# A hand-laid order of steps laid out anew, and the last half-tile stored from ScalarE's queue

## The reference

```
x = x + tanh(g_xattn) * autocorrelation(layernorm(x), ctx, ctx)
x = x + tanh(g_ffn)   * ffn(layernorm(x))

autocorrelation, per batch, 8 heads of 64 features, over the 64 tokens:
    corr = ifft(fft(q) * conj(fft(k))).real        # q = layernorm(x), k = v = ctx
    w, idx = top_k(corr, 8); w = softmax(w)        # per feature
    out[pos] = sum_i w[i] * v[min(idx[i] + pos, 63)]
ffn:
    out = (silu(x @ W_gate.T) * (x @ W_up.T)) @ W_down.T      # 512 -> 1792 -> 512, f16 weights
```

## Time and profile before

| | |
|---|---|
| Time, median of 3 runs | 213.95 us (213.7 to 213.95) |
| Profiled execution: first to last instruction | 212.1 us |
| Granted TensorE clock, mean | 1.000 |
| PE busy | 203.6 us (96%) |
| DVE, ACT, POOL busy | 135.7, 131.4, 122.4 us |

### The profile page before, as it was taken

How to read it: one execution, slowest core, us unless ns; L and a number is a source line. 1 busy time by engine, 2 the same in 40 slices (tenths; PEclk the granted TensorE clock), 3 DMA queues, 4 the chain that set the end, 5 groups by cost and what they waited for, 6 DMA issues and landing times.

```text
span 212.1 us, 6601 instructions
## 1 busy us (share of the span) xinstructions
PE 203.6 (96%) x2700; PEld 147.8 (70%) x2700; DVE 135.7 (64%) x408; ACT 131.4 (62%) x207; POOL 122.4 (58%) x151
## 2 busy tenths in 40 slices
...
DMA packets 20734, 17.89 MB, mean 84 GB/s; under 512 B 16096, under 2 KB 16992, under 8 KB 20320
## 3 DMA queue, kind: packets, MB, share of 16 engines
...
HBM read 10.65 MB, written 2.10 MB: 60 GB/s over the span
## 4 chain that ended last, share of the span: by engine, by line
PE 89%; DVE 5%; ACT 1%; DMA 1%; issue 1%; POOL 1%; DVEq 0%; POOLq 0%
PE psum L937 48%; PE psum L1121 23%; PE psum L920 6%; PE psum L1071 3%; PE psum L928 2%; PE psum L1056 2%; DMA x_sb<-x 1%; PE psum L1048 1%; PE psum L1014 1%; DVE top L792 1%; DVE probs L814 1%; DVE raw_stats L759 1%; PE psum L1016 1%; PE psum L1015 1%; DVE prod L782 1%
## 5 line engine op out<-in xcount | busy, mean ns | idle before, releaser
L937 PE MATMUL psum<-xt_hi,wu 128*128 128x128 f16 (+1 forms) x504 | 54.0, 213 | 0.0
L937 PE MATMUL psum<-xt_lo,wu 128*128 128x128 f16 (+1 forms) x504 | 54.0, 213 | 0.0
L937 PE MATMUL psum<-xt_hi,wg 128*128 128x128 f16 (+1 forms) x504 | 54.0, 213 | 0.0
L937 PE MATMUL psum<-xt_lo,wg 128*128 128x128 f16 (+1 forms) x504 | 53.9, 213 | 0.0
L632 POOL TENSOR_TENSOR hid_lo<-hid,hid_hi 128x512 f16<-128x512 f32 (+2 forms) x32 | 33.6, 1055 | 28.8 <-ACT hid_hi L750 28.7
L937 PEld LDWEIGHTS psum<-xt_hi,wg 128*128 128x128 f16 x504 | 44.8, 98 | 5.6 <-issue 5.0
L937 PEld LDWEIGHTS psum<-xt_hi,wu 128*128 128x128 f16 x504 | 45.0, 98 | 3.2 <-issue 2.4
L937 PEld LDWEIGHTS psum<-xt_lo,wu 128*128 128x128 f16 x504 | 45.1, 98 | 0.7
L937 PEld LDWEIGHTS psum<-xt_lo,wg 128*128 128x128 f16 x504 | 45.0, 98 | 0.6
L1121 PE MATMUL psum<-wd,hid_hi 128*128 128x512 f16 (+1 forms) x126 | 43.3, 356 | 0.0
L1121 PE MATMUL psum<-wd,hid_lo 128*128 128x512 f16 (+1 forms) x126 | 43.3, 355 | 0.0
...
## 6 DMA issues: line engine op xcount, KB each, us to landing
...
```

Source lines behind the costliest of these rows:

```text
L937: last = nc.tensor.matmul(psum[:, bank, a * n:(a + 1) * n], w[:, k, m * P:(m + 1) * P], xt[:, e, k, tok], start=(k == 0 and part == 0), st ...
```

## The change

The text `ORDER` is replaced. The set of steps is the same, with one more, `store_half:7`. PE's sequence is the same up to `kspec:2`; the other engines' sequences differ from the start. The beginning, one later place of the new text and both ends:

```diff
-warm:0 stats1:0 rstd1:0 kspec:0 q_norm:0 kcopy:0 qspec:0 kcopy:0.1 vspec:0 prod:0 stats1:1 lags:0 vcopy:0
-vcopy:0.1 prod:0.1 rstd1:1 kspec:1 max:0 lags:0.1 warm:0.1 sub:0 kcopy:1 sub8:0 match:0 exp8:0 exp:0 total:0
-vcopy:1 mask:0 max:0.1 kcopy:1.1 scale:0 sub8:0.1 wt:0 stats1:2 exp8:0.1 w_hi:0 match:0.1 gates:0 wspec:0
-q_norm:1 total:0.1 scales:0 sub:0.1 qspec:1 mix_prod:0 exp:0.1 mix_prod:0.2 mix:0 prod:1 mix:0.1 mask:0.1
-prod:1.1 residual:0 lags:1 k_hi:3 scale:0.1 rstd2:0 max:1 wt:0.1 rstd1:2 w_hi:0.1 sub:1 xn:0 wspec:0.1 match:1
+warm:0 stats1:0 rstd1:0 kspec:0 q_norm:0 kcopy:0 qspec:0 kcopy:0.1 vspec:0 prod:0 stats1:1 lags:0 vcopy:0 prod:0.1
+vcopy:0.1 rstd1:1 kspec:1 max:0 sub:0 q_norm:1 lags:0.1 sub8:0 match:0 exp8:0 exp:0 total:0 warm:0.1 vcopy:1 mask:0
+max:0.1 kcopy:1 scale:0 sub8:0.1 sub:0.1 exp8:0.1 wt:0 total:0.1 exp:0.1 match:0.1 w_hi:0 kcopy:1.1 wspec:0 stats1:2
+mask:0.1 gates:0 rstd1:2 qspec:1 mix_prod:0 mix_prod:0.2 mix:0 q_norm:2 scales:0 prod:1 mix:0.1 prod:1.1 scale:0.1
+lags:1 residual:0 wt:0.1 rstd2:0 max:1 w_hi:0.1 k_hi:3 sub:1 wspec:0.1 xn:0 match:1 xt:0 sub8:1 mix_prod:0.1 kspec:2
...
+residual:5 scale:6 gate:4.2 kcopy:7 w_rows_hi:6 rstd2:5 vcopy:7 up:4.1 h_hi:4 w_rows_lo:6 xn:5 up:4.2 hid:4.1
+tanh:4.2 q_lo:7 w_t:6.1 kcopy:7.1 silu:4.2 h_lo:4 w_t:6 gate:4.3 h_hi:4.1 hid:4.2 h_lo:4.1 up:4.3 store:3 tanh:4.3
...
-hid:7.2 up:7.3 h_hi:7.2 tanh:7.3 h_lo:7.2 down:7 silu:7.3 hid:7.3 h_hi:7.3 h_lo:7.3 down:7.1 down:7.2 down:7.3
-out:7 store:7
+silu:7.3 down:7 h_hi:7.2 h_lo:7.1 h_lo:7.2 hid:7.3 down:7.1 h_hi:7.3 h_lo:7.3 down:7.2 down:7.3 out:7 store:7
+store_half:7
```

The store of the right half leaves SP for ScalarE's queue, with a semaphore of its own:

```diff
                 if step == "store":
-                    for h, cols in enumerate(halves(p)):
-                        sp.wait_ge(out_ready, p + h + 1)
-                        sp.dma_start(outv[:, p:p + 1, cols], x_sb[:, p:p + 1, cols]).then_inc(stored, 16)
-            sp.wait_ge(stored, 16 * (PAIRS + 1))
+                    cols = halves(p)[0]
+                    sp.wait_ge(out_ready, p + 1)
+                    sp.dma_start(outv[:, p:p + 1, cols], x_sb[:, p:p + 1, cols]).then_inc(stored, 16)
+            sp.wait_ge(stored, 16 * PAIRS)
+            sp.wait_ge(half_stored, 16)
...
+                if step == "store_half":
+                    act.wait_ge(out_ready, PAIRS + 1)
+                    nc.scalar.dma_start(outv[:, p:p + 1, halves(p)[1]], x_sb[:, p:p + 1, halves(p)[1]])\
+                      .then_inc(half_stored, 16)
```

```diff
-    w_whole = sb("w_whole", [P, 2, D])
+    w_whole = v_turned[:, 0, :, :]
...
-    xt_hi = sb("xt_hi", [P, 2, KT, P], f16)
+    xt_hi = sb("xt_hi", [P, 4, KT, P], f16)
...
                 if step == "turn" and p in MOVED:
                     sp.wait_ge(v_copied, copies(p))
+                    if p == 2:
+                        sp.wait_ge(w_spectra, nth("wspec", 0, 1))
...
-                        if p >= 2:
-                            sp.wait_ge(up_done, STEPS * (p - 1))
+                        if p >= 4:
+                            sp.wait_ge(up_done, tokens_used(p))
...
                     if p >= 2:
-                        act.wait_ge(down_done, p - 1)
+                        act.wait_ge(down_step, hidden_free(p, n))
```

More of the change, by code:

```diff
@@ L19 @@
 MIX_UP = 8.0
-STEPS = 4
+GROUPS = tuple((p,) for p in range(PAIRS))
 SPANS = ((0, 4), (4, 8), (8, 12), (12, 14))
@@ L179 @@
[L179 to L208, removed]
@@ new lines @@
+exp8:1 exp:1 mix_prod:0.3 x_hi:0 mix:0.2 total:1 kcopy:2 mask:1 mix:0.3 x_lo:0 vcopy:2 scale:1 stats1:3 gate:0
+kcopy:2.1 residual:0.1 rstd1:3 k_hi:4 k_lo:3 qspec:2 w_rows_hi:1 tanh:0 w_t:1 up:0 rstd2:0.1 prod:2 p_hi:2 turn:1.3
+stats1:4 w_rows_lo:1 xn:0.1 gate:0.1 prod:2.1 p_lo:2 silu:0 p_hi:2.1 hid:0 xt:0.1 tanh:0.1 p_lo:2.1 up:0.1 w_t:1.1
+q_norm:3 silu:0.1 x_hi:0.1 rstd1:4 turn:2.3 lags:2 x_lo:0.1 hid:0.1 gate:0.2 max:2 k_lo:4 sub8:2 sub:2 exp8:2
+gate:0.3 match:2 exp:2 h_hi:0 q_hi:3 wspec:1 h_lo:0 total:2 h_hi:0.1 kspec:3 mask:2 tanh:0.2 mix_prod:1 up:0.2
@@ new lines @@
+scale:2 kcopy:3 mix_prod:1.1 mix_prod:1.2 h_lo:0.1 w_rows_hi:2 mix_prod:1.3 kcopy:3.1 mix:1 w_t:2 w_rows_lo:2
+silu:0.2 mix:1.1 vcopy:3 hid:0.2 q_lo:3 w_t:2.1 up:0.3 h_hi:0.2 residual:1 turn:3 h_lo:0.2 qspec:3 turn:3.1 wspec:2
+rstd2:1 prod:3 tanh:0.3 down:0 prod:3.1 p_hi:3 silu:0.3 p_hi:3.1 p_lo:3 mix_prod:2 k_hi:5 down:0.1 hid:0.3 xn:1
+p_lo:3.1 mix_prod:2.1 x_rows_hi:1 mix_prod:2.2 h_hi:0.3 lags:3 x_t:1 mix_prod:2.3 turn:3.2 h_lo:0.3 mix:2 max:3
+x_rows_lo:1 down:0.2 sub:3 x_t:1.1 match:3 exp:3 down:0.3 turn:3.3 mix:2.1 sub8:3 out:0 exp8:3 q_norm:4 kspec:4
@@ new lines @@
+p_lo:4.1 stats1:7 m_hi:3.1 down:1.3 m_lo:3 m_hi:3.2 lags:4 out:1 turn:4.1 m_lo:3.1 gate:2 mix_prod:3.3 max:4
+m_lo:3.2 gate:2.1 rstd1:6 sub8:4 sub:4 exp8:4 m_hi:3.3 match:4 exp:4 m_lo:3.3 q_hi:5 mix:3 turn:4.2 mix:3.1 q_lo:5
+mask:4 mix:3.2 total:4 kspec:5 tanh:2 residual:3 scale:4 up:2 kcopy:5 silu:2 w_rows_hi:4 up:2.1 turn:4.3 w_t:4
+w_rows_lo:4 hid:2 tanh:2.1 w_t:4.1 gate:2.2 h_hi:2 silu:2.1 vcopy:5 h_lo:2 hid:2.1 store:0 kcopy:5.1 gate:2.3
+rstd2:3 tanh:2.2 up:2.2 rstd1:7 xn:3 silu:2.2 h_hi:2.1 x_rows_hi:3 wspec:4 h_lo:2.1 hid:2.2 tanh:2.3 x_t:3 qspec:5
@@ new lines @@
+turn:5 silu:2.3 mix_prod:4 x_rows_lo:3 up:2.3 prod:5 h_hi:2.2 down:2 mix_prod:4.1 m_hi:4 x_t:3.1 h_lo:2.2 hid:2.3
+m_hi:4.1 prod:5.1 h_hi:2.3 mix_prod:4.2 p_hi:5 down:2.1 h_lo:2.3 q_norm:6 mix_prod:4.3 m_lo:4 m_hi:4.2 q_norm:7
+down:2.2 p_lo:5 p_hi:5.1 turn:5.1 p_lo:5.1 down:2.3 turn:5.2 m_lo:4.1 lags:5 out:2 gate:3 m_hi:4.3 max:5 m_lo:4.2
+q_hi:6 sub:5 m_lo:4.3 gate:3.1 sub8:5 tanh:3 match:5 exp:5 k_lo:6 turn:5.3 mix:4 mask:5 mix:4.1 exp8:5 q_hi:7
+total:5 mix:4.2 tanh:3.1 kspec:6 scale:5 residual:4 up:3 vcopy:6 q_lo:6 silu:3 kcopy:6 silu:3.1 up:3.1 w_rows_hi:5
```

183 lines of the change are left out of this document (116 added, 67 removed).

## The result

The changed kernel takes 216.53 us (median of 4 runs, 216.32 to 216.74) against 213.95 for the kernel before (4 runs, 213.7 to 214.47). The ratio is 1.0121, with a 95% interval of 1.0101 to 1.014. The forecast was 213.1, range 212.6 to 213.9, and it gave 0.08 to slower.

The account below looks back on a forecast made before the run. PE, busy 96% of the span, was taken as the bound, so only its waits and switches could be won. -0.22 - 0.4 - 0.33 + 0.1 = -0.85 us took the median from 213.95 to 213.1, range 212.6 to 213.9.

Parts of the forecast that it names:

- The head: Start up to `kspec:2`, where PE waits for DVE and ACT: `kspec:2` at 24.92 instead of 25.14, a gain of 0.22 us.
- The switches: PE's changes between matmul shapes after `kspec:2`: 40 instead of 44, about 0.1 us each, a gain of 0.4 us.
- The tail: Behind PE's last matmul: ACT issues the last output's right half at about 209.19, not SP at 209.52, gaining 0.33 us.
- The steady stretch: PE's reordered steps after the start: inputs' leads mostly 0.2 to 1 us, all fit, 0.1 us charged for the unseen.
- one landing of 2.5: Time for a weights' transpose to land, 2.5 us, in the sum of 8.45 against 8.7 us available before `wspec:6`.
- Slower: the transposes: Rival: slow issues and landings of the weights' transposes stall `wspec:6` 1.9 and `wspec:5` 1.7 us, giving 216.7; chance 0.10.

## Why the prediction was wrong

**The head** held: 24.84 for 24.92. In eleven traces with the new head `kspec:2` starts at 24.61 to 25.08, in three with the old head at 24.93 to 25.18 (four more, with slow f32 matmuls in the head as told above, reach it at 26.5 us and later).

**The switches** were priced about right: from `wspec:5` to the start of `down:7.3` PE took 90.84 us, for 90.8 with 0.1 a switch. No run has four switches fewer and nothing else, so the gain of 0.4 was not measured by itself.

**The tail** had the right size by the wrong reason, which is luck. 0.28 us came for 0.33 in the traces; the times are too coarse for it (the old order with the store on ScalarE: 1.0006 of before). The 0.36 delay of the second store was no matter of a second store on one queue, but of a place in SP's program. ScalarE's queue took the store from that place and from under the fetch, but record 80 then fell behind the last wait, where it cost 0.45. With both stores on SP in the new kernel the same place is covered, and the tail is 0.76 shorter than before. The Trainium skill's DMA: Bandwidth & Descriptors, "Issuing engines are not separate DMA queues", says that a second issuer saves only the sequencer's time; the trace agrees, with landings of 1.80 us from ScalarE and 1.78 from SP.

**The steady stretch** is the step that failed, the charge of 0.1. Its leads were about right: `wspec:6` 0.3 (PE went on 0.2 behind the landing, without a stall), `wspec:5` 0.5 (117.8 against 117.29 had it landed as usual). What failed is the price put into them, "one landing of 2.5", though the earlier trace rows held a landing of 3.6. The prediction set that value aside as an early one, beside the transfers of pairs 1 and 2. That one was early (issued at 34.06 us, with a fetch 0.07 behind it), but slow landings were not only early: the earlier trace rows show `w_lo` alone, and among the other turns of the same trace landings of 3.8, 4.1 and 4.2 us stand at 60, 67 and 160 us. PE needed those data 2.4, 6.7 and 3.4 us after they had landed, so they left no wait to see. The charge of 0.1 became 4.1 (3.9 without the two switches in it): 3.3 in three late landings of weights, 0.8 in two sums on VectorE and GpSimd that came out 0.3 to 0.5 short (`mix:1`, `lags:5`).

**The rival that came true** was "Slower: the transposes", with a chance of 0.10. It gave 216.7 and the measurement is 216.53, partly by luck: it had 1.9 at `wspec:6` and 1.7 at `wspec:5`; the trace has 2.07 at `wspec:5`, 0.6 each at `wspec:2` and `wspec:3`, nothing at `wspec:6`. Pairs 2 and 3 have the high rows first, so low rows first is not what made them late.

**What stays open.** Most of the delay is the fetch's own packet: the last pieces of a turn start when it ends. That they stand behind it on the same one of the 16 engines is my reading of these times; the trace names no engine for a packet. Why such a packet takes 0.9 to 1.7 us (q8) or up to 2.1 us (q14) is open, and so is why the landing is told 1.0 us behind the turn's last packets in the two turns shown above, where it is 0.3 us in a turn without a fetch. Open too is the cause of the 0.44 at SP's record 80. And the 0.5 before `mix:1` and 0.33 before `lags:5` were read from the traces only, not tried.
